# A Perceiver block with 6,272 keys: the second key half behind the second turns, value tiles elsewhere, moves in two parts, and the staging piece in front of the even context buffer

## The chip, the cores and the metric

The kernel runs on one core of one Trainium2 chip. The metric is the time of one execution in microseconds on the device; lower is better.

## The reference

A query of 64 rows of 512 numbers attends to 6,272 context rows of 512 (32 query heads of 128, 8 key and value heads). The result goes through a projection with bias, then through a block with weights kept as 4-bit codes with scales and low-rank parts (attention-like sum, gate and up, down), and a last layer with a Fourier transform of coefficients. The part that matters here, cut:

```python
q = (query @ Wq + bq).reshape(B, L, NKV, G, HDIM)
k_, v_ = jnp.split(kv @ Wkv + bkv, 2, axis=-1)
scores = jnp.einsum('blkgd,bmkd->bkglm', q, k) * scale
attn = jax.nn.softmax(scores, axis=-1)
o = jnp.einsum('bkglm,bmkd->blkgd', attn, v).reshape(B, L, NHEAD * HDIM)
return o @ Wo + bo
```

The 4-bit weights are expanded on the chip during the attention: codes become numbers (a maximum over straight lines), which are scaled and stored.

## The kernel before, in words

**Blocks and chunks.** The context is cut into NCH = 7 chunks of 896 keys (CT = 7 tiles of 128; two halves of 448). Each chunk passes 8 key heads; one chunk and one head make a block, i = 8 s + h, 56 in all (NB). A softmax that runs along with new maxima joins the chunks. Each float32 number is split in two parts (hi and lo), and each product is three matmuls (L86 to L90: hi by hi, hi by lo, lo by hi).

**The engines in a block.** Each engine has its own list, written out by hand, and runs it in order. PE (L944): the scores of the block in four pieces (two halves by two row tiles), the transposes ("turns") of the probabilities of the block before (turn_probs, four groups of up to two tiles), the keys of the next head in two halves (next_keys; the first into p_s, the second into p_kv), the product of values and probabilities (weigh_values, into p_o, in a part of tiles 0 to 3 and a part of 4 to 6), the value tiles of a pair of heads (value_tile, into the two banks of p_kv, 4 in even blocks and 3 in odd ones), and the turn of an output (turn_output). ACT (L1306) rounds what PE leaves in PSUM to the hi part, takes the exponentials (weigh), rounds pieces of the next chunk's context (round_ctx) and computes four of the eight lines of a weight tile. DVE (L1606) subtracts to get the lo parts (split_keys, split_values, split_probs), takes the score statistics, adds outputs, and merges lines (merge 0 to 5). GpSimd (POOL, L674) has the other lines, the lo part of context pieces (split_ctx), and joins and scales a weight tile (join). SP (L505) issues the loads.

**The moves.** The exponentials lie in probs. SP copies them by DMA to probs_r, one DMA for each of two row tiles, for the transposes to read (move_probs, L465). It first waits until all four turns of the block before have read probs_r (pt_psum, 4 i), and DVE may write probs again only when the copy has landed.

**The buffers.** The context of even chunks lies in ctx_even_hi and ctx_even_lo, that of odd chunks in ctx_odd_hi and ctx_odd_lo. While one chunk is worked on, the other buffer is filled in 16 pieces through one staging tile (ctx_st, 896 bytes in each partition), which lay between the two. ctx_piece (L71) says which piece goes at which of five places of a pair of blocks. The banks of p_kv are shared by keys, values and scores in turn. kv_number gives each use its number; PE waits on kv_split (DVE is through with that use), ACT and SP on kv_psum.

**The first blocks.** Blocks 0 to 2 also hold the rest of the query projection (query_product, query_turn on PE, query_out on ACT, finish_query on DVE) and the splitting of the key and value weights (round_wkv on ACT, split_wkv on DVE), with 1 MB loads of wq in the same queue.

## Time and profile before

| | us |
|---|---|
| median of 3 timed runs | 1011.46 |
| lowest and highest of them | 1010.75, 1011.51 |
| the profiled execution | 1011.92 |
| its span, first to last instruction | 1010.1 |
| PE busy in the span | 995.1 |
| DVE, ACT, POOL busy | 745.5, 586.5, 443.5 |

The profile is one execution. Each engine's busy time is the time in which it had an instruction under way. Matmuls overlap each other by their modelled ends, so that a busy PE can still stand for a short time: the distance from one start to the next tells more.

### The profile page before, as it was taken

What the parts mean: (1) busy time and instruction counts of PE and PEld (TensorE: products, weight loads), DVE (VectorE), ACT (ScalarE), POOL (GpSimd) and SP (SyncE); (2) the same over time, 40 slices, a digit from 0 to 9 for tenths busy, and PEclk for the clock granted to TensorE, in tenths of its full rate; (3) what the DMA queues carried; (4) which work ended last, traced back from release to release, by engine and by line L of the source; (5) the groups of instructions that cost most, each with busy time, mean ns of one, the idle gap of its engine ahead of it and who ended that gap; (6) DMA issues with size and microseconds to landing.
All of it is one profiled execution on the core that took longest, in us unless ns stands there. A gap on an engine that the chain in (4) does not pass through costs nothing.

```text
span 1010.1 us, 20355 instructions
## 1 busy us (share of the span) xinstructions
PE 995.1 (99%) x7083; PEld 921.6 (91%) x7083; DVE 745.5 (74%) x1680; ACT 586.5 (58%) x1254; POOL 443.5 (44%) x641
## 2 busy tenths in 40 slices
PE   8999999999999999999999999999999999999998
PEld 6779999999999999999999999999999999999744
DVE  5678878777777778777776778777777768676766
ACT  6466666666565656566565666656565655565431
POOL 2244553545534444345454444534444445333331
PEclk9999999999999999999999999999999999999999
DMA  9663333333324343243333334333333237464895
GB/s 324 226 223 130 124 129 132 109 134 108 124 94 134 119 135 135 96 134 108 131 106 116 114 132 137 116 119 108 130 107 134 97 124 249 158 223 153 235 351 166
DMA packets 90086, 149.59 MB, mean 148 GB/s; under 512 B 10529, under 2 KB 44977, under 8 KB 89985
## 3 DMA queue, kind: packets, MB, share of 16 engines
q1 hardware_dynamic: 88224, 146.42, 43.8%
q10 hardware_dynamic: 1424, 1.51, 0.4%
q8 instruction: 58, 0.95, 0.4%
q0 software_dynamic: 336, 0.35, 0.2%
q14 instruction: 44, 0.35, 0.1%
HBM read 82.97 MB, written 14.81 MB: 97 GB/s over the span
## 4 chain that ended last, share of the span: by engine, by line
PE 93%; DVE 3%; DMA 2%; issue 1%; SPq 0%; ACT 0%; DVEq 0%
PE p_kv L88 16%; PE p_kv L90 16%; PE p_kv L89 16%; PE p_s L88 7%; PE p_s L90 7%; PE p_s L89 6%; PE p_t L769 6%; PE p_o L88 5%; PE p_o L90 5%; PE p_o L89 5%; PE p_s L849 1%; PE p_ot L753 1%; DMA wkv_raw<-in_wkv 1%; PE p_o L783 1%; DMA probs_r<-probs 1%
## 5 line engine op out<-in xcount | busy, mean ns | idle before, releaser
L610 POOL TENSOR_SCALAR slots<-code 128x512 f32<-128x512 bf16 x232 | 148.7, 641 | 247.3 <-DVE slots L1466 162.4
L1210 ACT ACTIVATE pt_hi<-p_t 128x512 fp32r<-128x512 f32 x224 | 109.9, 542 | 113.6 <-PE p_t L769 107.9
L1466 DVE TENSOR_TENSOR slots<-slots 128x512 f32<-128x512 f32 x232 | 170.0, 733 | 1.6 <-POOL slots L610 1.5
L1239 ACT ACTIVATE slots<-code,drop_and_offsets 128x512 f32<-128x512 bf16 x232 | 158.6, 713 | 8.1 <-POOL code L606 4.1
L1198 ACT ACTIVATE v_hi<-p_kv 128x256 fp32r<-128x256 f32 x196 | 75.2, 384 | 139.6 <-PE p_kv L90 138.7
L630 POOL TENSOR_TENSOR slots<-slots 128x512 f32<-128x512 f32 x58 | 77.0, 1327 | 158.2 <-DVE slots L1466 158.2
L1430 DVE TENSOR_TENSOR pt_lo<-p_t,pt_hi 128x512 fp32r<-128x512 f32 x224 | 128.7, 614 | 5.9 <-ACT pt_hi L1210 4.9
L1415 DVE TENSOR_TENSOR v_lo<-p_kv,v_hi 128x256 fp32r<-128x256 f32 x196 | 83.1, 424 | 67.6 <-ACT v_hi L1198 64.8
L88 PE MATMUL p_kv<-wkv_hi,ctx_even_hi 128*128 128x256 f32 x448 | 129.1, 288 | 0.2 <-DVE v_lo L1415 0.2
L89 PE MATMUL p_kv<-wkv_lo,ctx_even_hi 128*128 128x256 f32 x448 | 126.0, 281 | 0.0
L90 PE MATMUL p_kv<-wkv_hi,ctx_even_lo 128*128 128x256 f32 x448 | 126.0, 281 | 0.0
L1280 ACT ACTIVATE probs<-probs,mins 128x896 f32<-128x896 f32 x112 | 115.5, 1038 | 0.0
L88 PE MATMUL p_o<-pt_hi,v_hi 128*128 128x256 f32 x392 | 111.2, 284 | 2.2 <-issue 2.2
L1417 DVE SCALAR_TENSOR_TENSOR k_lo<-p_kv,bk_sb,k_hi 128x448 fp32r<-128x448 f32 x56 | 38.3, 684 | 100.6 <-ACT k_hi L1198 100.6
L90 PE MATMUL p_o<-pt_hi,v_lo 128*128 128x256 f32 x392 | 111.1, 283 | 0.0
L89 PE MATMUL p_o<-pt_lo,v_hi 128*128 128x256 f32 x392 | 110.8, 283 | 0.0
L88 PE MATMUL p_kv<-wkv_hi,ctx_odd_hi 128*128 128x256 f32 x336 | 97.0, 289 | 0.0
L90 PE MATMUL p_kv<-wkv_hi,ctx_odd_lo 128*128 128x256 f32 x336 | 94.9, 283 | 0.0
L89 PE MATMUL p_kv<-wkv_lo,ctx_odd_hi 128*128 128x256 f32 x336 | 94.4, 281 | 0.0
L1198 ACT ACTIVATE k_hi<-p_kv,bk_sb 128x448 fp32r<-128x448 f32 x56 | 35.6, 635 | 91.4 <-PE p_kv L90 91.4
L88 PEld LDWEIGHTS p_kv<-wkv_hi,ctx_even_hi 128*128 128x128 f32 x448 | 84.5, 189 | 1.1 <-issue 1.1
L89 PEld LDWEIGHTS p_kv<-wkv_lo,ctx_even_hi 128*128 128x128 f32 x448 | 84.6, 189 | 0.0
(261 smaller groups left out, 2717.7 us busy)
## 6 DMA issues: line engine op xcount, KB each, us to landing
probs_r<-probs SPq DMA_DIRECT2D x110, 448.0 KB, 3.6
code<-in_codes SPq DMA_DIRECT2D x58, 256.0 KB, 3.8
scale<-in_scales SPq DMA_DIRECT2D x114, 128.0 KB, 3.1
expanded_weights<-slots SPq DMA_DIRECT2D x56, 256.0 KB, 2.1
ctx_st<-in_ctx_t SPq DMA_DIRECT2D x96, 112.0 KB, 3.0
ring_hi<-expanded_weights SPq DMA_DIRECT2D x22, 256.0 KB, 5.9
ring_lo<-expanded_weights SPq DMA_DIRECT2D x22, 256.0 KB, 6.0
wq_hi<-in_wq SPq DMA_DIRECT2D x4, 1024.0 KB, 7.2
```

The costliest lines, as they stand in the source:

```text
L88: nc.tensor.matmul(out, hi, rhi, start=start, stop=False)
L89: nc.tensor.matmul(out, hi, rlo, start=False, stop=False)
L90: return nc.tensor.matmul(out, lo, rhi, start=False, stop=stop)
L610: nc.gpsimd.tensor_scalar(slots[:, slot, :], code16[:], LINES[j][0], LINES[j][1], ALU.mult, ALU.add).then_inc(pool_lines, 1)
L630: nc.gpsimd.tensor_tensor(slots[:, 0, :], slots[:, 0, :], slots[:, 4, :], ALU.subtract).then_inc(joined, 1)
L1198: nc.scalar.activation(dst, src, ACT.Identity, bias=0.0 if bias is None else bias).then_inc(kv_rounded, 1)
L1210: nc.scalar.activation(pt_hi[:, at:at + n, :].rearrange("p t q -> p (t q)"), p_t[:, c % 2, 0:n * ROWS], ACT.Copy).then_inc(pt_rounded, 1)
L1239: nc.scalar.activation(slots[:, slot, :], code16[:], ACT.Identity, bias=offsets[:, k:k + 1], scale=LINES[j][0]).then_inc(act_lines, 1)
L1280: nc.scalar.activation(probs[:, r, :], probs[:, r, :], ACT.Exp, bias=mins[:, h, r, now:now + 1], scale=-1.0, accum_out=rowsum[:, h % 4, r: ...
L1415: nc.vector.tensor_tensor(dst, src, hi.bitcast(F32), ALU.subtract).then_inc(kv_split, 1)
L1430: nc.vector.tensor_tensor(pt_lo[:, at:at + n, :].rearrange("p t q -> p (t q)"), p_t[:, c % 2, 0:n * ROWS], pt_hi[:, at:at + n, :].rearrang ...
L1466: nc.vector.tensor_tensor(slots[:, slot, :], slots[:, slot, :], slots[:, other, :], ALU.max).then_inc(merged, 1)
```

## The change

1. **Staging tile.** ctx_st is allocated in front of ctx_even_hi and no longer behind ctx_even_lo. The even buffers move up by 896 bytes; the odd ones stay.
2. **Order.** On PE the second key half follows the second pair of turns directly. The three value tiles of odd blocks go ahead of these turns, the four of even blocks to the end of the block. ACT and DVE follow the same order. The scores' second half then waits for the last use of the banks (last_kv). turn_output(0) and add_output(0, 0) go from block 2 to block 3.
3. **Moves in two parts.** move_probs copies columns 0 to 511 (front, when the first two turns before have read them) and columns 512 to 895 (back, when all have), each with its own semaphore.
4. **Pieces and lines.** The context pieces go at other places of ACT's, POOL's and SP's lists, and in chunk 0 two pieces are moved ahead; POOL's first two lines are separated by a piece; PE waits for the new context in four steps.

The diff, cut to its core:

```diff
@@ ctx_piece
-        piece = (0, 1, PIECES, PIECES, 2)[place]
+        piece = (0, 1, PIECES, 2, 3)[place]
+    elif pair == 1 and place < 2:
+        piece = (4, PIECES)[place]
@@ kv_number
-                uses = keys[:1] + tiles[:SPLIT_TILE] + keys[1:] + tiles[SPLIT_TILE:]
+                uses = keys + tiles if i % 2 == 0 else keys[:1] + tiles + keys[1:]
...
+            last_kv[i] = len(kv_number) - 1
@@ v_bank
+            return (t + 1) % 2 if i % 2 == 0 else t % 2
@@ move_probs
                 if i > 0:
+                    sp.wait_ge(pt_psum, 4 * i - 2)
+                for r in range(RT):
+                    sp.wait_ge(exp_ready, 2 * i + 1 + r)
+                    sp.dma_start(probs_r[:, r, FRONT].bitcast(F32), probs[:, r, FRONT]).then_inc(front_moved, 16)
+                if i > 0:
                     sp.wait_ge(pt_psum, 4 * i)
                 for r in range(RT):
-                    sp.wait_ge(exp_ready, 2 * i + 1 + r)
-                    sp.dma_start(probs_r[:, r].bitcast(F32), probs[:, r]).then_inc(probs_moved, 16)
+                    sp.dma_start(probs_r[:, r, BACK].bitcast(F32), probs[:, r, BACK]).then_inc(back_moved, 16)
@@ SP, a pair of blocks
                     load(0)
                     move_probs(n)
+                    load(1)
                     codes_of(n + 2)
-                    load(1)
@@ POOL, a pair of blocks
                     last_lines(n)
-                    narrow(n + 1)
+                    if n == 0:
+                        narrow(1)
                     split(0)
+                    if n > 0:
+                        narrow(n + 1)
                     add_rowsum(n, 2 * pair)
                     split(1)
                     join(n)
+                    first_line(n + 1)
                     split(2)
-                    first_lines(n + 1)
+                    second_line(n + 1)
@@ PE scores
-                    pe.wait_ge(kv_split, (LAST_KV if i == NB - 1 and c == 1 else use) + 1)
+                    pe.wait_ge(kv_split, (last_kv[i - 1] if c == 1 else kv_number["k", i - 1, 0]) + 1)
@@ PE block_work
+                if i == 3:
+                    turn_output(0)
                 turn_probs(i - 1, 0)
                 turn_probs(i - 1, 1)
...
-                if h + 1 == NKV:
-                    pe.wait_ge(ctx_split, PIECES * (s + 1))
                 next_keys(i, h, half, 0)
                 weigh_values(i - 1, 0, SPLIT_TILE)
                 if i == 2:
                     query_product(7)
+                if i % 2 == 1:
+                    for t in value_tiles(i):
+                        value_tile(i, h, half, t)
                 turn_probs(i - 1, 2)
                 turn_probs(i - 1, 3)
                 if i > 2:
                     turn_output(i - 2)
-                for t in value_tiles(i)[:SPLIT_TILE]:
-                    value_tile(i, h, half, t)
                 next_keys(i, h, half, 1)
                 weigh_values(i - 1, SPLIT_TILE, CT)
-                if i == 2:
-                    turn_output(0)
+                if i % 2 == 0:
+                    for t in value_tiles(i):
+                        if i == 2 and t == 2:
+                            query_turn(7)
+                        value_tile(i, h, half, t)
@@ ACT block_work
                 round_probs(i - 1, 0)
                 round_probs(i - 1, 1)
+                if h % 2 == 1:
+                    round_ctx(s, h, half, 2)
+                elif h >= 2:
+                    round_ctx(s, h - 2, half, 4)
...
                 round_probs(i - 1, 2)
                 round_probs(i - 1, 3)
+                round_ctx(s, h, half, 0 if h % 2 == 0 else 3)
...
                 round_keys(i, h, 1)
                 if i == 1:
                     round_wkv(3)
+                    query_out(6)
                     lines(i + 1, 0, 2)
@@ DVE block_work, even blocks
+                    for t in value_tiles(i):
+                        split_values(i, t)
+                        if t < 3:
+                            merge(i, 3 + t)
+                        if t == 1 and i < NKV - 2:
+                            split_wkv(h + 2)
+                        if t == 2 and i == 2:
+                            finish_query(7)
```

In odd blocks DVE splits tiles 4 to 6 ahead of split_probs 2 and 3, with merges 2 to 4 between them; in chunk 0 split_wkv follows split_probs.

## Rows read from the trace of the kernel before

**Rows 1.** The page, busy time of each engine.

```profile
PE 995.1 (99%) x7083; PEld 921.6 (91%) x7083; DVE 745.5 (74%) x1680; ACT 586.5 (58%) x1254; POOL 443.5 (44%) x641
```

**Rows 2.** Waits of PE: releaser, us in total, times, longest us.

```profile
PE p_o L88 <- issue: 2.2, 2, 1.3
...
PE p_kv L88 <- DVE v_lo L1415: 0.2, 1, 0.2
```

**Rows 3.** Windows, one pair of steady blocks.

```profile
core 0: us, PE busy (x) PEld busy (x) DVE busy (x) ACT busy (x) POOL busy (x), PEclk, DMA share, GB/s
457.00:489.50 32.50, 32.50 (x233) 31.35 (x232) 24.35 (x56) 20.13 (x46) 15.74 (x24) 1.00 0.37 124
```

**Rows 4.** Windows of an even and an odd chunk, instructions that touch wkv_hi; columns without POOL.

```profile
294.50:424.50 130.00, 77.67 (x352) 57.26 (x352) 0.00 (x0) 0.00 (x0) 1.00 0.36 120
424.50:554.50 130.00, 77.79 (x352) 57.22 (x352) 0.00 (x0) 0.00 (x0) 1.00 0.36 120
```

**Rows 5.** Groups by form of the whole span, first key half.

```profile
L89 PE MATMUL p_s<-ctx_even_lo,wkv_hi 128*128 128x448 f32 x128 | 47.0, 367 | 0.0
...
L89 PE MATMUL p_s<-ctx_odd_lo,wkv_hi 128*128 128x448 f32 x96 | 34.9, 363 | 0.0
```

**Rows 6.** Timeline at the boundary of blocks 54 and 55.

```profile
932.82 0.38 ACT L1198 ACTIVATE v_hi<-p_kv 128x256 fp32r<-128x256 f32 x1 [1.03 <-PE p_kv L90]
...
934.04 0.36 PE L88 MATMUL p_s<-k_hi,q_hi 128*128 128x448 f32 x1
...
934.25 0.38 ACT L1198 ACTIVATE v_hi<-p_kv 128x256 fp32r<-128x256 f32 x1 [1.04 <-PE p_kv L90]
...
934.66 0.42 DVE L1415 TENSOR_TENSOR v_lo<-p_kv,v_hi 128x256 fp32r<-128x256 f32 x1 [1.00 <-ACT v_hi L1198]
...
935.14 0.19 PEld L88 LDWEIGHTS p_kv<-k_hi,q_hi 128*128 128x128 f32 x1
935.25 0.37 PE L88 MATMUL p_kv<-k_hi,q_hi 128*128 128x448 f32 x1
```

**Rows 7.** Timeline of DVE in block 2.

```profile
79.68 0.68 DVE L1466 TENSOR_TENSOR slots<-slots 128x512 f32<-128x512 f32 x1
80.28 1.22 DVE L1586 TENSOR_TENSOR wkv_lo<-wkv_raw,wkv_hi 128x1024 fp32r<-128x1024 f32 x1
81.42 0.48 DVE L1568 TENSOR_TENSOR q_f<-p_ot,bq_sb 128x128 f32<-128x128 f32 x2
...
83.58 0.41 DVE L1415 TENSOR_TENSOR v_lo<-p_kv,v_hi 128x256 fp32r<-128x256 f32 x1
```

**Rows 8.** Timeline of PE in blocks 1 and 2.

```profile
58.84 1.95 PE L783 MATMUL p_ot<-wq_hi,xt 128*64 128x256 f32 x16 [0.30 <-DMA wq_hi<-in_wq]
...
64.37 0.38 PE L793 MATMUL p_ot<-ident,q_part 128*128 128x128 f32 x2
65.44 0.88 PE L769 MATMUL p_t<-ident_r,probs_r 128*128 128x128 f32 x8 [0.69 <-DMA probs_r<-probs]
...
68.54 0.37 PE L90 MATMUL p_s<-ctx_even_hi,wkv_lo 128*128 128x448 f32 x1
70.17 0.36 PE L88 MATMUL p_o<-pt_hi,v_hi 128*128 128x256 f32 x1 [1.26 <-issue]
```

**Rows 9.** Timeline of the DMA issues of SP.

```profile
51.63 0.63 SPq L484 DMA_DIRECT2D wq_lo<-in_wq  x1
56.04 1.15 SPq L471 DMA_DIRECT2D probs_r<-probs  x2
...
58.60 1.35 SPq L434 DMA_DIRECT2D ctx_st<-in_ctx_t  x1
```

**Rows 10.** Timeline of ACT in block 2.

```profile
66.37 0.39 ACT L1228 ACTIVATE ctx_odd_hi<-ctx_st 128x224 fp32r<-128x224 f32 x1 [4.95 <-DMA ctx_st<-in_ctx_t]
...
68.16 1.07 ACT L1210 ACTIVATE pt_hi<-p_t 128x512 fp32r<-128x512 f32 x2
```

**Rows 11.** Landing times of the moves (tile probs_r) between 100 and 850 us.

```profile
DMA to landing us min/median/max: 2.8/3.6/5.0
```

More of the change, by code:

```diff
@@ L139, in perceiver_block @@
               w_base, b_base, enc, coefs, mask, fourier, ident_in, out, ident, acc, denom, mins, bk_sb, bv_sb, wkv_hi,
[L140 removed]
+              wkv_lo, q_hi, q_lo, ctx_st, even_hi, even_lo, where, sem, sb, psum)
         phase1.close()
@@ L617, in first_lines, with second_line @@
                 line(0, 0)
+            def second_line(n, first=False):
                 if not first:
@@ L1321, in block_work @@
+                if h % 2 == 1:
+                    if i > 1:
+                        lines(i + 1, 0, 2)
+                round_keys(i, h, 1)
                 if i == 1:
                     round_wkv(3)
-                if h % 2 == 1:
-                    round_ctx(s, h, half, 3)
-                for n, t in enumerate(value_tiles(i)[:SPLIT_TILE]):
-                    round_values(i, t)
-                    if n == 1 and i < NKV - 2:
-                        round_wkv(h + 2)
-                    elif n == 1:
-                        lines(i + 1, 0, 1)
-                    if n == 2:
-                        lines(i + 1, 0 if i < NKV - 2 else 1, 2)
-                    if h % 2 == 0 and n == 2:
-                        round_ctx(s, h, half, 1)
@@ L1335, in block_work @@
-                if i == 1:
-                    lines(i + 1, 0, 2)
-                round_keys(i, h, 1)
-                if i == 1:
-                    query_out(6)
-                for t in value_tiles(i)[SPLIT_TILE:]:
-                    round_values(i, t)
-                round_ctx(s, h, half, 2 if h % 2 == 0 else 4)
+                    query_out(6)
+                    lines(i + 1, 0, 2)
+                if h % 2 == 0:
+                    for t in value_tiles(i):
+                        round_values(i, t)
+                        if t == 0 and i < NKV - 2:
+                            round_wkv(h + 2)
+                        if t == 1:
+                            if i >= NKV - 2:
+                                lines(i + 1, 0, 1)
+                            round_ctx(s, h, half, 1)
+                        if t == 2:
+                            lines(i + 1, 0 if i < NKV - 2 else 1, 2)
@@ L1620, in block_work @@
                 split_keys(i, h, 0)
-                merge(i, 2)
-                split_probs(i - 1, 2)
-                split_probs(i - 1, 3)
-                if i == 1:
-                    split_wkv(3)
+                if h % 2 == 1:
+                    tiles = value_tiles(i)
+                    for n in range(CT - SPLIT_TILE):
+                        if tiles:
+                            split_values(i, tiles[n])
+                        if n == 0:
+                            merge(i, 2)
+                        elif n == 1:
+                            merge(i, 3)
+                            merge(i, 4)
+                    split_probs(i - 1, 2)
+                    split_probs(i - 1, 3)
+                    if 1 < i < NKV - 2:
+                        split_wkv(h + 2)
+                    else:
+                        merge(i, 5)
+                else:
+                    split_probs(i - 1, 2)
+                    split_probs(i - 1, 3)
                 if i == 6:
@@ L1631, in block_work @@
                     invert(h - 2)
-                tiles = value_tiles(i)[:SPLIT_TILE]
-                for n in range(3):
-                    if n < len(tiles):
-                        split_values(i, tiles[n])
-                    merge(i, 3 + n)
-                if 1 < i < NKV - 2:
-                    split_wkv(h + 2)
-                if i == 2:
-                    finish_query(7)
-                for t in tiles[3:]:
-                    split_values(i, t)
-                split_keys(i, h, 1)
-                if i == 2:
-                    add_output(0, 0)
-                for t in value_tiles(i)[SPLIT_TILE:]:
-                    split_values(i, t)
+                if h % 2 == 0:
+                    merge(i, 2)
+                split_keys(i, h, 1)
+                if i == 1:
+                    split_wkv(3)
+                if h % 2 == 1:
+                    if 1 < i < NKV - 2:
+                        merge(i, 5)
+                else:
+                    for t in value_tiles(i):
+                        split_values(i, t)
+                        if t < 3:
+                            merge(i, 3 + t)
+                        if t == 1 and i < NKV - 2:
+                            split_wkv(h + 2)
+                        if t == 2 and i == 2:
+                            finish_query(7)
             def last_block():
```

61 lines of the change are left out of this document (35 added, 26 removed).

## The prediction

> **What bounds the kernel now.** I read the page first: PE is busy 995.1 of 1010.1 us [rows 1]. No other engine is near its limit, so a change of order can gain only what PE loses. Then I asked what PE waits for: 2.2 us "issue" before p_o and 0.2 us for a v_lo [rows 2], and 0.7 us for the move of the probabilities [rows 8]. A matmul's modelled end hides a part of each wait, so for the rest I read starts. In the steady part PE is busy all of the time, 32.50 of 32.50 us for a pair of blocks at the upper clock level [rows 3]. So what can be won or lost lies (a) in the first blocks, where PE does stand, (b) in new waits that the order might bring 25 times over, (c) in how fast the matmuls follow each other.
>
> **The moved address (even buffer 896 B further on).** No instruction changes. Its only possible effect is on the pace. The chunk from 294.50 uses the even buffer, that from 424.50 the odd one, which keeps its address: for the matmuls that touch wkv_hi PE is busy 77.67 us in the one and 77.79 in the other [rows 4]. The buffers do differ, but by 0.12 us a chunk, with keys dearer in even (367 against 363 ns for the same form [rows 5]) and so something else dearer in odd. If even comes to behave as odd in all: 3.5 chunks by 0.12, +0.4 us. In the keys alone: 4 ns on 24 matmuls in each of 28 blocks, -2.7 us. I take 0, nearest to the whole-chunk rows.
>
> **The second key half behind the second turns.** 12 matmuls of 448 columns now follow transposes instead of value tiles (in odd blocks value tiles, transposes, keys). The first half already follows transposes, and its pace is what rows 5 show: 363 to 367 ns. One matmul behind the transposes is slow either way, the first value matmul before, the first key matmul now, so that price moves and does not go. The pace of 54 blocks by 12 such matmuls can change by the spread of 4 ns at most, 648 by 4 = 2.6 us up or down. I take -1.0: less than half of it, to the better side, since 363 is had behind transposes in the odd chunks.
>
> **Value tiles elsewhere: the new wait in steady blocks.** In even blocks the four tiles come last, and the next block's second-half scores write the banks that the last tiles used, so PE waits until DVE has read them (last_kv). The trace has this very pattern once, at the last block: first score matmul at 934.04, ACT rounds the tile at 934.25, DVE splits it at 934.66 for 0.42, to 935.08; the weight load comes at 935.14 and its matmul at 935.25 [rows 6], six steps of 0.20 behind 934.04. The load goes 0.1 us later than it could and nothing is lost. Elsewhere DVE and ACT must be free at that moment. Tiles come 1.43 us apart (932.82 to 934.25 in rows 6); DVE has a split and a merge for each, 0.42 + 0.68 = 1.10 us, and ACT a rounding of 0.38 and one line (0.7 us; two in chunk 0). Cost 0; from the other side 0.1 us for an exposed weight load, 25 times, +2.5 us.
>
> **Where it does cost: block 3.** In block 2 DVE also has split_wkv(4), 1.22 us, now behind tile 1, and finish_query(7), from 81.42 to 83.58, between tiles 2 and 3; it splits tile 3 only at 83.58 [rows 7]. Before, 12 key matmuls (2.4 us), 9 of p_o (1.1) and 6 of the scores (1.2) stood between tile 3 and the first need of its bank; now the last 1.2 alone. From the end of tile 0 (T): DVE splits and merges to T+1.6, splits tile 1 at T+2.0, merges and does split_wkv to T+4.2, tile 2 and its merge to T+5.1, finish_query to T+6.6 (1.5 us where POOL leaves it alone) or 7.3, tile 3 to T+7.0 or 7.7. PE would be at the second half at T + 3 x 1.43 + 1.2 = T+5.5. Block 3 stands 1.5 to 2.2 us; I take 1.7. Block 4 has a split_wkv but no finish_query: +0.1.
>
> **Moves in two parts, and the piece ahead of them.** PE loses in block 2: query_turn's transposes at 64.37, those of the probabilities at 65.44, where 0.1 to 0.2 is due: 0.9 us. And 68.54 to 70.17 where 0.20 is due: 1.4 us [rows 8]. The move was issued at 56.04, behind the last MB of wq (51.63), the context piece at 58.60 [rows 9]. ACT stood 4.95 us for this piece, until 66.37, and turned to the probabilities at 68.16 [rows 10]: the second stall is ACT's. After, load(3) takes that piece ahead of the moves, near 52.3, and the front part goes when exp is done, near 54.5. But the queue serves in order: wq_hi was there for PE at 58.84 [rows 8]; at 0.35 MB a us (3 us a MB, an estimate from the page's highest slices) the next MB is there at 61.8, the piece at 62.0, the front part at 63.5, the back part at 64.8. ACT now stands for the piece in front of the second keys, whose matmuls are over at 58.5: k_hi starts at 62.3, k_lo ends at 63.6, and PE, which wants it at 63.1, stands 0.5 us. On DVE split_wkv(3) ends at 65.1 and the score statistics start there, not at the 65.4 of before; ACT is through with the probabilities 1 us earlier, and the p_o of 70.17 starts at about 69.1. Gain 1.1 us; 2.3 if both stalls went, 0 if they only change places.
>
> **The steady moves.** The back part of an odd block waits for turns that now come behind three value tiles: 2.4 (scores) + 0.6 (turns) + 2.4 (keys) + 1.4 (p_o) + 4.3 (tiles) + 0.6 = 11.7 us into the block, issued by 12.9. A whole move lands in 2.8 to 5.0 us, median 3.6 [rows 11]: at 16.5, at worst 17.9. DVE writes the second half of probs 1.9 us into the next block, at 15.5 + 1.9 = 17.4, and its split of the probabilities has 0.7 us to spare before PE wants it. Codes, piece, tile_out and scales behind it in SP's queue shift by 4 us, with over 3 us of room in each. Cost 0; the other side, 0.3 us in each of 25 odd blocks, 7.5 us, holds only if the landings of now were all at the slow end. The Trainium skill, "DMA: Bandwidth & Descriptors", "Anatomy of one DMA", gives each DMA a fixed part of about 2 us, which speaks against two parts; no row here shows it alone. By it, were the two parts paid one behind the other, the landing would be 18.5 and each odd block would wait 0.4 us.
>
> **Smaller ones.** In block 7 the last context piece of chunk 0 is split at about 5.0 us, where PE asks for it: +0.2. The v_lo wait of block 50 [rows 2] is a backlog of DVE; tiles 3.5 us later are past it: -0.3. In the last pair join(54) and the ring loads behind it are 3 us later, their slots read over 10 us later: 0.
>
> **Sum.** -1.1 (block 2) + 1.7 (block 3) + 0.1 + 0.2 - 0.3 - 1.0 (pace) = -0.4. The profiled execution took 1011.92 us (span 1010.1), 0.46 over the timed median of 1011.46. So 1011.5 there, 1011.06 as a median: 1011.0. A measurement of this kernel can tell about 0.2%, 2 us, from no change.
>
> **Rivals.** *Faster, by pace*: the keys alone take the better pace, by the address (-2.7) and by the order (-2.6 in place of -1.0): at most -4.7, half as much is likelier, 1008.6. For it: the pace depends on something (rows 5). Against: whole chunks differ by 0.12 us (rows 4). By the Trainium skill, "SBUF — State Buffer", "Who interferes with whom", PE never waits on another engine's accesses; by that rule an address matters in nothing.
> *Slower, by the tail of the tiles*: if DVE or ACT come to the last tile later than in rows 6, the 0.1 us of room is gone and every further 0.1 us costs 2.5 us; 0.1 beyond it gives 1013.5, 0.15 gives 1015. For: the room is little. Against: 1.10 us of work in 1.43.
> *Slower, by the back part* landing late: 0.1 us in each odd block is 2.5 us, 1013.5 and more. It decides from a landing at 18.1 on.
> *No reach*: block 2's stalls come back in another place and block 3 stands 2.2: with a pace of 0, 0 + 2.2 + 0 = +2.2 on 1011.46 less 0.3, 1013.4.
>
> **Chances.** The forecast 0.32 and half of the last rival's 0.20 stay within 0.2%; the faster rival 0.34; the tail of the tiles 0.10, the back part 0.04, half of the last rival 0.10. So faster 0.34, same 0.42, slower 0.24. The range takes 1008.0, beyond the faster rival's likelier half, to 1014.5.
>
> **What the next profile would show.** Block 3 with a gap of 1.5 to 2.2 us ahead of its second-half scores, released by DVE's v_lo. In block 2 no DMA wait of p_t, and 1 us or less ahead of p_o. ACT idle for ctx_st once, 3 to 5 us, until about 62. Steady pairs at 32.4 to 32.6 us with PE busy throughout: one over 32.7 says that the tile tail or the back part waits. Key matmuls of the even chunks at 363 ns would speak for the address. I am wrong if pairs change by over 0.1 us, or if block 3 does not stand.

## The result, and the profile after

The kernel after takes 1016.57 us (median of 6 executions, 1015.16 to 1018.66); the kernel before takes 1011.49 beside it (6 executions, 1010.07 to 1012.81). The ratio is 1.0054, 95% interval 1.0042 to 1.0065: 5 us slower, where 1011.0 was forecast and 1014.5 was the upper end. The profiled execution, the longest of the six, took 1018.66 us with a span of 1016.9 (first to last instruction).

The profile page's engine row and PE's waits answer to [rows 1] and [rows 2]. PE is busy 2.8 us more than in the kernel before, and a single wait for v_lo takes 2.8 us.

```profile
PE 997.9 (98%) x7083; PEld 922.4 (91%) x7083; DVE 756.2 (74%) x1680; ACT 584.9 (58%) x1254; POOL 457.7 (45%) x641
```

```profile
PE p_kv L90 <- DVE v_lo L1445: 3.1, 2, 2.8
...
PE p_o L90 <- issue: 1.6, 2, 1.0
...
PE p_s L90 <- DVE probs L1484: 0.9, 1, 0.9
```

To place the loss I took, for each block, the time from its first matmul (`p_s<-k_hi,q_hi` in the timeline of PE) to that of the next block. The table has these lengths in us for the kernel before, the kernel after, and four kernels of the experiments below. Each column is one profiled execution. In the columns spread and last_mended the clock fell early in block 0, which took 1.6 us more for it.

```
block        before   after  join_late  spread  all_mended_no_shift  last_mended
0             29.16   29.14      29.14   30.72                29.15        30.72
1 and 2       36.19   36.39      37.05   38.56                34.16        34.66
3             15.60   20.28      16.62   15.71                15.72        15.76
4             17.02   16.92      16.92   17.37                17.44        17.03
5             15.52   16.12      16.10   15.52                15.52        15.59
7             15.48   15.90      15.90   15.91                15.78        15.51
8 to 49      682.84  683.88     683.89  683.86               682.73       682.97
50            17.42   17.02      17.02   17.02                16.97        16.97
```

From before to after the two profiled spans differ by 6.8 us, more than the medians (5.1): block 3 has 4.7 of it, blocks 8 to 49 together 1.0, block 5 0.6, block 7 0.4, the start and blocks 1 and 2 0.4; block 50 gives 0.4 back.

Block 3 in the timeline of PE. The last matmul of the first score half starts at 85.21 and the first of the second half at 88.36, where 0.20 is due. What is over the due distance from one start to the next is called a stand here: this one has 2.95 us, and DVE's v_lo ends it. Behind it the matmuls follow at 0.37 us instead of 0.20.

```profile
85.21 0.36 PE L92 MATMUL p_s<-k_hi,q_lo 128*128 128x448 f32 x1
88.36 0.74 PE L90 MATMUL p_kv<-k_hi,q_hi 128*128 128x448 f32 x1 [2.79 <-DVE v_lo L1445]
88.90 0.57 PE L91 MATMUL p_kv<-k_lo,q_hi 128*128 128x448 f32 x1
89.27 0.57 PE L92 MATMUL p_kv<-k_hi,q_lo 128*128 128x448 f32 x1
```

The windows of the same stretch say why: the granted clock is 0.51 from 88.30 to 91.00, which is the lower level (1.2 GHz), behind the stand. Of the block's 4.68 us more, 2.95 are the stand. The other 1.73 are nearly all the low clock: in whole_moves, an experiment below, the same stand came without the fall, and the block took 1.47 us less (18.81). The first of these rows is a steady pair, to set beside [rows 3]; the columns are those named there.

```profile
463.50:496.10 32.60, 32.60 (x233) 31.32 (x232) 24.89 (x56) 20.04 (x45) 16.77 (x24) 1.00 0.37 124
84.20:104.50 20.30, 17.51 (x114) 16.40 (x113) 16.90 (x36) 11.66 (x25) 8.29 (x11) 0.92 0.26 82
85.00:88.30 3.30, 0.57 (x3) 0.19 (x1) 3.23 (x6) 1.16 (x2) 2.93 (x3) 1.00 0.00 0
88.30:91.00 2.70, 2.64 (x8) 2.27 (x9) 1.72 (x7) 0.00 (x0) 0.20 (x1) 0.51 0.56 190
```

What DVE did before that v_lo, to set beside [rows 7]: the steps come in the forecast order, but the seventh query's finish (q_f, q_hi, q_lo) takes from 84.72 to 87.89, 3.2 us.

```profile
82.65 1.22 DVE L1616 TENSOR_TENSOR wkv_lo<-wkv_raw,wkv_hi 128x1024 fp32r<-128x1024 f32 x1
83.79 0.42 DVE L1445 TENSOR_TENSOR v_lo<-p_kv,v_hi 128x256 fp32r<-128x256 f32 x1
84.12 0.68 DVE L1496 TENSOR_TENSOR slots<-slots 128x512 f32<-128x512 f32 x1
84.72 0.48 DVE L1598 TENSOR_TENSOR q_f<-p_ot,bq_sb 128x128 f32<-128x128 f32 x2
85.23 1.17 DVE L1604 CAST q_hi<-q_f 128x256 fp32r<-128x256 f32 x1
86.43 1.54 DVE L1606 TENSOR_TENSOR q_lo<-q_f,q_hi 128x256 fp32r<-128x256 f32 x1
87.89 0.41 DVE L1445 TENSOR_TENSOR v_lo<-p_kv,v_hi 128x256 fp32r<-128x256 f32 x1
```

The merge at 84.12 is what POOL's join had waited for. The two steps of the join lie on q_hi and q_lo:

```profile
84.98 1.27 POOL L639 TENSOR_TENSOR slots<-slots 128x512 f32<-128x512 f32 x1 [6.66 <-DVE slots L1496]
86.43 1.26 POOL L648 TENSOR_TENSOR slots<-slots,scale 128x512 f32<-128x512 f32 x1 [0.18 <-POOL slots L639]
```

In blocks 1 and 2, ACT stands for ctx_st once, as forecast, and PE takes the probabilities without a wait for their move; but a `split_wkv` on DVE takes 2.30 us beside POOL's join, and the score statistics behind it come late. POOL's steps are at 64.24 and 65.72, the second with 2.04 us instead of 1.26. These rows answer to [rows 8] and [rows 10].

```profile
62.42 0.39 ACT L1246 ACTIVATE ctx_odd_hi<-ctx_st 128x224 fp32r<-128x224 f32 x1 [5.54 <-DMA ctx_st<-in_ctx_t]
```

```profile
64.32 2.30 DVE L1616 TENSOR_TENSOR wkv_lo<-wkv_raw,wkv_hi 128x1024 fp32r<-128x1024 f32 x1 [0.27 <-ACT wkv_hi L1290]
```

```profile
64.11 0.47 PE L90 MATMUL p_kv<-k_hi,q_hi 128*128 128x448 f32 x1 [0.35 <-DVE k_lo L1447]
67.31 0.44 PE L90 MATMUL p_s<-ctx_even_hi,wkv_hi 128*128 128x448 f32 x1 [0.88 <-DVE probs L1484]
```

### The profile page after: what moved, and what is told of

It reads as the page before. It is cut to its first block, busy times and chain, and to the rows that moved or that the text cites. A ratio compares the mean times of both kernels' runs of the same rounds, so it can differ in the third digit from the quotient of the medians.

```text
span 1016.9 us, 20498 instructions
## 1 busy us (share of the span) xinstructions
PE 997.9 (98%) x7083; PEld 922.4 (91%) x7083; DVE 756.2 (74%) x1680; ACT 584.9 (58%) x1254; POOL 457.7 (45%) x641
## 4 chain that ended last, share of the span: by engine, by line
PE 92%; DVE 3%; DMA 2%; issue 1%; ACT 1%; SPq 1%; POOL 0%; DVEq 0%; POOLq 0%; ACTq 0%
PE p_kv L90 16%; PE p_kv L92 16%; PE p_kv L91 15%; PE p_s L90 7%; PE p_s L91 6%; PE p_s L92 6%; PE p_t L785 6%; PE p_o L90 5%; PE p_o L92 5%; PE p_o L91 4%; PE p_s L865 1%; PE p_ot L769 1%; DMA wkv_raw<-in_wkv 1%; DMA ctx_st<-in_ctx_t 1%; PE p_o L799 1%
## 5 line engine op out<-in xcount | busy, mean ns | idle before, releaser
L617 POOL TENSOR_SCALAR slots<-code 128x512 f32<-128x512 bf16 x232 | 154.5, 666 | 137.5 <-DVE slots L1496 78.1
L1496 DVE TENSOR_TENSOR slots<-slots 128x512 f32<-128x512 f32 x232 | 173.0, 746 | 22.5 <-POOL slots L617 22.5
L1257 ACT ACTIVATE slots<-code,drop_and_offsets 128x512 f32<-128x512 bf16 x232 | 162.3, 718 | 21.7 <-POOL slots L639 18.3
L90 PE MATMUL p_kv<-wkv_hi,ctx_even_hi 128*128 128x256 f32 x448 | 126.8, 283 | 0.0
L90 PE MATMUL p_kv<-wkv_hi,ctx_odd_hi 128*128 128x256 f32 x336 | 94.8, 282 | 0.0
L1500 DVE SCALAR_TENSOR_TENSOR slots<-slots 128x512 f32<-128x512 f32 x116 | 84.8, 731 | 0.0
L92 PEld LDWEIGHTS p_kv<-wkv_hi,ctx_even_lo 128*128 128x128 f32 x448 | 84.0, 187 | 0.0
```

The costliest lines, as they stand in the source:

```text
L90: nc.tensor.matmul(out, hi, rhi, start=start, stop=False)
L92: return nc.tensor.matmul(out, lo, rhi, start=False, stop=stop)
L617: nc.gpsimd.tensor_scalar(slots[:, slot, :], code16[:], LINES[j][0], LINES[j][1], ALU.mult, ALU.add).then_inc(pool_lines, 1)
L1257: nc.scalar.activation(slots[:, slot, :], code16[:], ACT.Identity, bias=offsets[:, k:k + 1], scale=LINES[j][0]).then_inc(act_lines, 1)
L1496: nc.vector.tensor_tensor(slots[:, slot, :], slots[:, slot, :], slots[:, other, :], ALU.max).then_inc(merged, 1)
L1500: nc.vector.scalar_tensor_tensor(slots[:, slot, :], slots[:, slot, :], 0.0, slots[:, other, :], ALU.max, ALU.max).then_inc(merged, 1)
```

## The experiments

**How the times are to be read.** The executions of one kernel differ in their mean granted clock. Of the 23 of the kernel before that ran beside the first four experiments, 11 had 1.000 (median 1010.70) and 12 had 0.998 or 0.999 (1012.48). The traces show where the clock falls: in nine of the fourteen it is at its lower level for some 3.5 us between 18 and 24 us, and block 0 takes 30.6 to 31.3 us instead of 29.15. Elsewhere it falls only at a stand. The intervals below hold this scatter, so a difference under 1 us is read from the blocks of the traces, not from the medians. That also holds for the kernel after: 4 of its 6 executions had a clock of 1.000 (median 1016.28), so the low clock of block 3 is not in every one, and against the 1010.70 above the loss is 5.6 us without it.

**Theory and rivals.** Theory: DVE has a backlog at the end of block 2 (wkv split, query finish beside POOL's join), the stand of block 3 is that backlog and makes the clock fall; smaller waits of the same kind cost blocks 5 and 7; the rest is 1.0 us of pace, that is, of how fast the matmuls follow each other where nothing stands. Rivals: the moves in parts or the new order cost something everywhere; or the moved address does.

**query_last and join_late: the order on DVE, and POOL beside it.**

```diff
@@ query_last, DVE block_work
-                        if t == 2 and i == 2:
+                        if t == 3 and i == 2:
                             finish_query(7)
@@ join_late, DVE block_work
-                        if t < 3:
+                        if t < (2 if i == 2 else 3):
                             merge(i, 3 + t)
+                        if t == 3 and i == 2:
+                            merge(i, 5)
```

> The kernel after, with the seventh query's finish (turn with bias, rounding, low half, on DVE) moved in block 2 from behind the third value tile's split to behind the fourth's. Theory 1 (block 3's stand is the fourth tile's low half coming late behind that finish, and the low clock after it is the stand's result): the stand of 2.95 us shrinks to under 0.3 us, no stretch of block 3 has a granted clock near 0.5, block 3 goes from 20.3 us to 15.7 to 16.2, and the kernel to 1012.0 to 1012.8. Theory 2 (the time is lost all over, in the steady blocks' order and the moves in two parts; block 3 is one incident among others): the stand goes but blocks lose elsewhere, and the kernel stays at 1015 or more.

> The kernel after, with the last merge of block 2's lines (which releases POOL's join) moved behind the fourth tile's split; the seventh query's finish stays ahead of that split. It tells how much of the 3.2 us that the finish took is POOL working beside it. If POOL slows it: the finish takes 1.5 to 1.8 us, the stand in block 3 is 0.9 to 1.4 us instead of 2.95, and the kernel takes 1013.3 to 1014.8 (by whether the clock still falls behind a stand of 1 us). If the finish is as long alone: stand 2.5 us or more, 1016.0 to 1016.6.

Measured: query_last 1015.96 (ratio 1.0036, 1.0025 to 1.0048); join_late 1015.33 (1.0035, 1.0023 to 1.0048). By the ratios both give back nearly 2 us, by the medians 0.9 and 1.5, each less than forecast. Among executions with a clock of 1.000 the medians are 1015.43 and 1013.95 against 1016.28 of the kernel after. In join_late the finish takes 1.27 us instead of 3.2, with q_hi at 0.29 and q_lo at 0.43, and the stand is 0.37 us, less than I had expected:

```profile
84.51 0.48 DVE L1598 TENSOR_TENSOR q_f<-p_ot,bq_sb 128x128 f32<-128x128 f32 x2
85.02 0.29 DVE L1604 CAST q_hi<-q_f 128x256 fp32r<-128x256 f32 x1
85.35 0.43 DVE L1606 TENSOR_TENSOR q_lo<-q_f,q_hi 128x256 fp32r<-128x256 f32 x1
85.69 0.42 DVE L1445 TENSOR_TENSOR v_lo<-p_kv,v_hi 128x256 fp32r<-128x256 f32 x1
```

So POOL's join cost DVE 2.0 us there; the other 0.6 us that the stand lost is the merge itself, which the edit also takes from in front of the finish. The Trainium skill, "SBUF — State Buffer", "Who interferes with whom", says that a DVE instruction with two SBUF inputs, or a cast in a two-port mode, shares a port pair with GpSimd and blocks as a whole, while one with at most one SBUF input outside these modes does not; the trace agrees: q_f, with an input from PSUM, stays at 0.48 in both kernels.

In query_last block 3 still takes 16.80 us. The stand moved: PE comes to the output's matmuls before the probabilities are ready, since the score statistics start only behind the finish. It is 1.02 us from start to start where 0.20 is due.

```profile
92.06 0.36 PE L92 MATMUL p_s<-ctx_even_hi,wkv_lo 128*128 128x448 f32 x1
93.08 0.36 PE L90 MATMUL p_o<-pt_hi,v_hi 128*128 128x256 f32 x1 [0.66 <-issue]
```

**stage_alone and order_no_shift: the address by itself, in both orders.** The first is the kernel before with ctx_st allocated in front of ctx_even_hi; the second is the kernel after with ctx_st behind ctx_even_lo.

> The kernel before with one edit: the staging piece lies in front of the even context buffer, so all buffers behind it keep their order but the even pair starts one piece later. Theory A (the pair's address sets the pace): even chunks' and odd chunks' key projections get one spacing, and the time moves by up to 1 us. The prediction's sign: 1010.3 to 1010.8; the sign that the kernel after shows in blocks 8 to 49 (1.0 us longer): 1012.0 to 1012.8. Theory B (the order inside the blocks sets it, the address nothing): 1011.3 to 1011.7, and even and odd chunks still differ as before.

> The kernel after with the staging piece back behind the even buffer; new order and moves in two parts stay. Theory A (address sets the pace, and the shift cost the 1 us of blocks 8 to 49): 1015.3 to 1015.9, even and odd chunks differ again as in the kernel before. Theory B (the order cost it): 1016.4 to 1016.8, blocks 8 to 49 sum to 683.9 us as with the shift. The stand of block 3 is there in both.

Measured: stage_alone 1010.72 (0.9995, 0.9985 to 1.0004); order_no_shift 1015.55 (1.0038, 1.0025 to 1.0050). Neither interval can tell the address, so the pace is read from the traces.

order_no_shift shows something else as well. Its stand in block 3 is 1.86 us, not 2.95, with the same steps in the same order: q_hi is slow beside the join as before, but q_lo takes 0.42 us, and it is POOL's second step that is the longer one (1.57 instead of 1.26). The clock stays at 1.00 there, and the block takes 17.74 us, 2.15 more than before.

```profile
85.97 1.17 DVE L1604 CAST q_hi<-q_f 128x256 fp32r<-128x256 f32 x1
87.17 0.42 DVE L1606 TENSOR_TENSOR q_lo<-q_f,q_hi 128x256 fp32r<-128x256 f32 x1
```

```profile
87.16 1.57 POOL L648 TENSOR_TENSOR slots<-slots,scale 128x512 f32<-128x512 f32 x1 [0.18 <-POOL slots L639]
```

The first matmuls of blocks 8 and 50 give the pace of the 42 blocks between. The kernel before, then after, stage_alone and order_no_shift:

```profile
164.41 0.36 PE L88 MATMUL p_s<-k_hi,q_hi 128*128 128x448 f32 x1
...
847.25 0.36 PE L88 MATMUL p_s<-k_hi,q_hi 128*128 128x448 f32 x1
```

```profile
170.44 0.36 PE L90 MATMUL p_s<-k_hi,q_hi 128*128 128x448 f32 x1
...
854.32 0.36 PE L90 MATMUL p_s<-k_hi,q_hi 128*128 128x448 f32 x1
```

```profile
163.27 0.36 PE L88 MATMUL p_s<-k_hi,q_hi 128*128 128x448 f32 x1
...
845.63 0.36 PE L88 MATMUL p_s<-k_hi,q_hi 128*128 128x448 f32 x1
```

```profile
168.54 0.37 PE L90 MATMUL p_s<-k_hi,q_hi 128*128 128x448 f32 x1
...
851.43 0.36 PE L90 MATMUL p_s<-k_hi,q_hi 128*128 128x448 f32 x1
```

That is 682.84 and 683.88 us, 682.36 and 682.89. The shift takes 0.5 us off in the old order and adds 1.0 in the new one; the new order alone adds nothing (0.05). Other traces repeat the figures: with the new order and the shift five more have 683.79 to 683.90 (where the moves stay in two parts), with the new order and no shift two more have 682.73 and 682.97; for the shift in the old order there is one trace only. So theory A, that the address changes the pace, holds in each run, but not with one sign. With the shift all chunks are alike, a pair of blocks at 32.49 us in the old order and 32.57 in the new; without it their lengths differ from chunk to chunk (15.47 to 15.64 for an odd block of the kernel before). The odd chunks change too, though their own buffers stay where they are (from 130.04 to 129.97 us a chunk in the old order, from 130.16 to 130.26 in the new). Why the order decides what the shift gives, no run here tells.

**whole_moves and parts_alone: the moves in two parts.** whole_moves is the kernel after with each row tile moved by one transfer of 896 columns behind the fourth turn, with one semaphore for both halves of the statistics and for all turns; parts_alone is the kernel before with move_probs, DVE's wait and PE's wait as in the kernel after.

> The kernel after with each block's exponents moved in one part again, one transfer for each row tile; order and shift stay. Theory (the parts are hidden, as the prediction had it): within 0.5 us of the kernel after, 1016.1 to 1017.0. Rival (the parts cost DVE and SP time, or keep the even and the odd blocks' first transposes waiting): 1015.5 or less. Rival of the other sign (the new order needs the front part early, because the score statistics of the next block overwrite it): transposes or statistics wait by 0.2 us or more in each block, 1025 or more.

> The kernel before with the moves in two parts and nothing else. Theory (hidden, and its gain is the 0.7 us that the transposes of block 2 stood for the moved exponents): 1010.8 to 1011.8, and that stand is gone or under 0.2 us. Rival (four issues instead of two on SP delay the loads behind them): 1012.5 or more, with longer stands for query weights or context pieces in blocks 1 and 2.

Measured: whole_moves 1020.28 (1.0089, 1.0072 to 1.0106); parts_alone 1011.93 (1.0005, 0.9996 to 1.0014). The parts cost nothing alone, and in the new order they are needed: without them the median is 3.7 us higher. Part of that is clock, since none of the six executions of whole_moves had 1.000 and four of the kernel after did. The trace shows a mechanism in blocks 6 and 8, 1.5 us together, and nothing of it in the blocks behind; its execution was one of the shorter ones (1018.97), and where the rest goes in the longer ones stays open. The statistics, which overwrite the probabilities, wait 1.33 us for the whole move, and PE then stands before the output's matmuls, 0.64 us over its due distance in block 6, 0.70 in block 8.

```profile
138.69 0.62 DVE L1480 TENSOR_SCALAR_CACHE_REDUCE probs<-p_s 128x448 f32<-128x448 f32 x1 [1.33 <-DMA probs_r<-probs]
```

**pieces_back: the context pieces of the first two pairs.**

```diff
@@ ctx_piece
     elif pair == 0:
-        piece = (0, 1, PIECES, 2, 3)[place]
-    elif pair == 1 and place < 2:
-        piece = (4, PIECES)[place]
+        piece = (0, 1, PIECES, PIECES, 2)[place]
```

> The kernel after with the context pieces of the first two pairs in the places that they had before (the third piece is loaded in the last place of the first pair, the next two in the second pair's first). Theory (the earlier third piece keeps the one staging buffer, and ACT stands 5.5 us for it, which makes the low keys of block 1 late by 0.5 us and the scores' statistics by 1.0): blocks 1 and 2 together are 0.5 to 1.0 us shorter than the 36.4 of the kernel after, 1015.6 to 1016.1. Rival (it is the query weights' and probabilities' transfers that are late, whatever the pieces): 1016.4 to 1017.0.

Measured: 1016.03 (1.0047, 1.0031 to 1.0063), too wide an interval for 0.5 us. In the trace blocks 1 and 2 take 34.36 us instead of 36.39. That is more than forecast, and not all of it need be the pieces: the wait for the query weights at the end of block 1 differs between traces whose kernels do the same up to there (0.81 us over the due distance in the kernel after, 1.12 in join_late, 1.25 in query_last, 2.57 in spread, none in order_no_shift, where only an address is different), and in this trace there is none. Block 3 takes 20.68 us here: POOL's split of a context piece falls on the wkv split, which takes 1.70 us instead of 1.22, the stand grows to 3.42 us, and the clock falls with it.

**spread: the backlog taken apart.** In block 2 PE's query turn, ACT's wkv rounding and DVE's finish go ahead of the first tile, and the wkv split behind the first tile's split; in block 4 the two wkv steps do the same.

```diff
@@ DVE block_work, even blocks
+                    if i == 2:
+                        finish_query(7)
                     for t in value_tiles(i):
                         split_values(i, t)
+                        if t == 0 and i < NKV - 2:
+                            split_wkv(h + 2)
                         if t < 3:
                             merge(i, 3 + t)
-                        if t == 1 and i < NKV - 2:
-                            split_wkv(h + 2)
-                        if t == 2 and i == 2:
-                            finish_query(7)
```

> The kernel after with three of block 2's steps moved ahead of its value tiles (the wkv rounding on ACT and the seventh query's turn on PE ahead of the first tile, its finish on DVE ahead of the first tile's split, the wkv split behind that one; the wkv steps so in block 4 too). They fall into DVE's idle stretches of 1.6 us (78.7 to 80.3) and ACT's of 1.9 in the trace of the kernel after. Theory 1 (a backlog of DVE at the end of blocks 2 and 4 makes the stands of blocks 3 and 5, and moving one step of it behind the last tile only moved the stand to the output's matmuls): block 3 takes 15.6 to 15.9 us, block 5 15.5 to 15.7, and the kernel is 3.5 to 4.2 us shorter than the kernel after, 1012.3 to 1013.1. Theory 2 (the later score statistics and exponents of the new order would stand in the way in any case): block 3 stays at 16.6 or more and the kernel above 1014.

Measured: 1015.10 (1.0037, 1.0024 to 1.0050), above the 1012.3 to 1013.1 of theory 1; by the time alone it would speak for theory 2. The blocks do what theory 1 said, block 3 at 15.71 and block 5 at 15.52, while block 4 loses 0.45: its fourth tile now waits for DVE. The total does not follow in this execution (1017.67, the longest of five), because blocks 1 and 2 take 38.56. The wait for the query weights was 2.57 us over the due distance (2.42 in the row), and the clock fell behind it, in the windows 0.75 and then 0.65:

```profile
62.61 2.65 PE L799 MATMUL p_ot<-wq_hi,xt 128*64 128x256 f32 x16 [2.42 <-DMA wq_hi<-in_wq]
```

```profile
62.40:65.00 2.60, 2.39 (x16) 1.26 (x16) 0.00 (x0) 0.00 (x0) 0.00 (x0) 0.75 0.96 359
65.00:68.00 3.00, 3.00 (x15) 2.77 (x14) 1.36 (x2) 2.57 (x5) 1.72 (x4) 0.65 0.38 133
```

The run by itself therefore doesn't settle the sum; the next two do.

**all_mended and all_mended_no_shift: all causes taken away.** These are spread and pieces_back together, and this edit on POOL for block 7; the second has ctx_st behind the even buffer as well.

```diff
@@ POOL, a pair of blocks
                     join(n)
-                    first_line(n + 1)
-                    split(2)
+                    if s == 0 and pair == 3:
+                        split(2)
+                        first_line(n + 1)
+                    else:
+                        first_line(n + 1)
+                        split(2)
                     second_line(n + 1)
```

> The kernel after (shift kept) with three edits together: block 2's and 4's steps spread as in the run spread; the context pieces of the first two pairs placed as before, as in pieces_back; and in the first chunk's last pair POOL's third context split again ahead of the first line (it ended at 159.68 us and released block 7's keys 0.25 us late). Theory (the named incidents and 1.0 us of pace are all there is): blocks 3, 5 and 7 at 15.7, 15.5 and 15.5 us, blocks 1 and 2 together 34.4 to 36.2, the steady blocks 8 to 49 still at 683.7; 1011.0 to 1012.3. Rival (a general cost of the new order that no incident shows): 1013 or more.

> The same with the staging piece back behind the even buffer. Theory (in the new order the shift costs pace, in the old one it gives some): blocks 8 to 49 at 682.9 instead of 683.7, the rest as in all_mended; 0.8 to 1.0 us less, 1010.0 to 1011.4. Rival (the pace of the profile is hidden or made up elsewhere): the same time as all_mended.

Measured: all_mended 1012.31 (1.0006, 0.9997 to 1.0015), all_mended_no_shift 1011.30 (0.9992, 0.9983 to 1.0000), beside the same executions of the kernel before. So the named incidents and the shift are the loss: of 5 us, 4.3 to 4.8 go with the first kernel and 1.0 to 1.4 more with the second, whose blocks 8 to 49 take 682.73 us against 683.90 in the first. Only the POOL edit did nothing. Block 7 stays at 15.90: POOL's split waits for ACT's ctx_odd_hi, which ACT rounds in block 7 and rounded at the end of block 6 before.

**stands: what an idle time costs when it is made on purpose.**

```diff
@@ the kernel before
+AGAIN = {12: 3, 20: 4, 28: 6, 36: 8, 44: 10}
@@ DVE split_kv
                 dve.wait_ge(kv_rounded, use + 1)
+                for _ in range(again):
+                    nc.vector.tensor_reduce(scrap[:, len(used):len(used) + 1], src, AX_X, ALU.min)
+                    used.append(use)
@@ DVE split_keys
+                         AGAIN.get(i, 0) * c)
```

> The kernel before, with idle stands made on purpose in five steady even blocks: DVE reduces the key projection once more 3, 4, 6, 8 and 10 times ahead of the low keys of blocks 12, 20, 28, 36 and 44 (into columns that nobody reads), so that the next block's second half of scores stands for them, by an estimate of 0.5 us for each reduction less a cover of 0.9 us: 0.6, 1.1, 2.1, 3.1 and 4.1 us. It tells from which stand on the granted clock falls. Theory (the stand itself makes the clock fall, from about 2.5 us, as behind the 2.95 us of block 3): granted clock near 0.5 for some 3 us behind the two longest, 1.00 behind the three shorter; blocks 37 and 45 lose 1.4 to 1.8 us more than their stand; 1023 to 1027. Rival (the clock falls for what came before, the slow start of blocks 1 and 2, and a stand amid steady work costs its own length): 1.00 throughout, 1021 to 1023.

Measured: 1029.70 (1.0171, 1.0156 to 1.0186). The stands are 0.91, 1.44, 2.51, 3.57 and 4.63 us, 2 us more in all than estimated, and the kernel is above the 1027 of the theory. The blocks that hold them are longer than the odd blocks on either side (15.60 or 15.49) by 0.99, 1.62, 2.59, 6.05 and 6.62: the first three lose their stand and 0.1 to 0.2 us, the last two 2.5 and 2.0 us beyond it. The windows behind the third and the fourth stand show the clock at 1.00 in the one case and at 0.50, its lower level, in the other. There it had fallen before PE resumed at 648.11, and it was low until 653.5; behind the fifth stand PE resumed at 785.43 and the clock was low until 790.0. That is 5.4 and 4.6 us of work at half the clock, against 3.4 in block 3 of the kernel after, and the losses follow it.

```profile
514.80:518.00 3.20, 3.20 (x21) 2.95 (x21) 3.13 (x12) 1.56 (x4) 0.00 (x0) 1.00 0.01 2
644.30:648.00 3.70, 0.41 (x2) 0.02 (x1) 3.70 (x8) 0.56 (x2) 1.23 (x2) 0.82 0.55 174
648.00:651.50 3.50, 3.39 (x15) 3.03 (x15) 2.48 (x10) 0.28 (x1) 0.00 (x0) 0.50 0.00 0
651.50:655.00 3.50, 3.50 (x15) 3.16 (x14) 2.73 (x6) 2.96 (x7) 0.47 (x1) 0.72 0.00 0
```

So a stand amid steady work does bring the clock down, and the rival falls. The Trainium skill, "TensorE: Matmul & The Clock Gate", "HAM oscillation — how this bites in real kernels", says that waits of PE between stretches of matmuls throttle it and that each next stretch then starts at the lower clock; these rows agree. How long a stand has to be is not settled. The clock stayed up behind 2.51 us here, 1.86 in order_no_shift and 2.95 in whole_moves; it fell behind 2.57 in spread, 2.95 in the kernel after and 3.42 in pieces_back. So stands between 2.5 and 3 us did both.

**last_mended.** It takes up the two losses left in all_mended_no_shift: in block 4 the wkv split goes ahead of the first tile's split, and ACT rounds the last context piece of the first chunk at the end of block 6.

```diff
@@ DVE block_work, even blocks
                     if i == 2:
                         finish_query(7)
+                    elif i < NKV - 2:
+                        split_wkv(h + 2)
                     for t in value_tiles(i):
                         split_values(i, t)
-                        if t == 0 and i < NKV - 2:
+                        if t == 0 and i == 2:
                             split_wkv(h + 2)
@@ ACT block_work
                 if h % 2 == 1:
-                    round_ctx(s, h, half, 2)
+                    if i != 7:
+                        round_ctx(s, h, half, 2)
...
                     lines(i + 1, 3, 4)
+                    if i == 6:
+                        round_ctx(s, h, half, 2)
```

> The kernel of all_mended_no_shift with the two losses that its profile still shows taken up: in block 4 the wkv split goes ahead of the first value tile's split (there the fourth tile's matmuls stood 0.41 us for it; block 4 took 17.44 us), and ACT rounds the first chunk's last context piece at the end of block 6, as the kernel before does, instead of in block 7 (where POOL's split waited for ACT and PE's keys 0.25 us for POOL; that block took 15.78 us). Theory: block 4 at 17.0, block 7 at 15.5, in all 0.5 to 0.7 us less than all_mended_no_shift beside the same kernel before: a ratio of 0.9984 to 0.9990. Rival (the ACT step at the end of block 6 delays the score exponents of block 7 by as much): block 7 or 8 gains nothing, ratio 0.9990 to 0.9996.

Measured: 1009.43 us, 0.9980 of the kernel before beside it (1011.68), interval 0.9971 to 0.9989, a little better than forecast. This version beats both kernels, and at a clock of 1.000 as well (1009.42 against 1011.43). Blocks 4 and 7 are at 17.03 and 15.51, as forecast. Against the kernel before the gain lies in blocks 1 and 2 (34.66 us against 36.19) and block 50 (0.4); the steady blocks have none, and block 3 is 0.2 us longer. The windows of blocks 3, 4 and 7 show PE busy throughout at the upper clock:

```profile
83.70:99.50 15.80, 15.80 (x114) 15.07 (x113) 13.35 (x31) 11.30 (x24) 8.35 (x11) 1.00 0.35 114
99.50:116.50 17.00, 17.00 (x123) 16.28 (x123) 14.36 (x30) 10.30 (x23) 9.79 (x13) 1.00 0.37 126
149.00:164.50 15.50, 15.50 (x111) 14.83 (x110) 11.73 (x29) 9.90 (x22) 8.27 (x11) 1.00 0.37 117
```

## Why the prediction was wrong

**The term of block 3** is the step that failed, by size: 1.7 us was taken, 1.5 to 2.2 allowed, and block 3 grew by 4.7. The mechanism, its place and its releaser were right. Two things were missing. The finish was counted at 1.5 us, or 2.2 with POOL beside it, from [rows 7], where only q_lo was slow; where POOL's join would fall in the new order was not worked out. The merge that releases it comes just ahead of the finish, so the join fell on both steps that POOL can slow: 3.2 us, and 1.27 with the join elsewhere, as join_late shows. And the cost of a stand was taken as its length, when this one brought the lower clock, some 1.5 us more. Neither is in every trace of the same order: block 3 grew by 2.15 us in order_no_shift, where the join slowed one step only, inside the range that was allowed, and by 3.2 in whole_moves, where the clock stayed up. So the range held one of the outcomes that this order can have, and not the dearer ones.

**The term of blocks 1 and 2**, -1.1, came out at +0.2. The k_lo wait (0.5 forecast), ACT's long stand (until 62.42; 62.0 forecast) and the shorter stand before p_o were right. Two sizes were not. The wkv split was put at its length of 1.22 and took 2.30 beside POOL, which made the statistics start at 66.5 instead of the 65.1 named, and PE stand 0.88 us; and the query weights came 0.3 us later. pieces_back speaks for the moved context pieces as a part of it, without settling how much.

**The pace**, -1.0, came out at +1.0 over blocks 8 to 49, with the wrong sign. The order gave nothing, where I had -1.0, and the shift 1.0 more, where I had 0. The evidence that I used, 363 against 367 ns for one form [rows 5], was too small and too partial to give a sign. Nor does an address matter in nothing, as the prediction drew from a rule on engines waiting for each other's accesses; with the shift alone the pace changed in both orders. In the kernel after that form has 364 in even chunks and 365 in odd ones.

**Block 4's wkv split**, +0.1: the backlog shows in block 5, whose second score half waits 0.48 us for block 4's last tile; the split took 1.69 us, not 1.22, beside POOL's context split. Block 5 lost 0.6 and block 4 gained 0.1. **Block 7**, +0.2: +0.4, of which 0.25 stands at the place named. **Block 50**, -0.3: -0.4. **The tail of the tiles** and **the steady moves**, both 0: right; a steady pair takes 32.57 us with PE busy throughout, inside the 32.4 to 32.6 named. The 0.4 us for each odd block, worked out for two parts paid one behind the other, does not appear; the section of the Trainium skill from which the prediction took the fixed part ("DMA: Bandwidth & Descriptors", "Anatomy of one DMA") states it for transfers that GpSimd issues, and these are SP's. But parts_alone and whole_moves show that the two parts were not neutral in the new order: without them its median is 3.7 us higher.

So the sum of -0.4 was off by 3.0 us in block 3 (1.5 of it the clock, in some executions), 1.3 in blocks 1 and 2, 2.0 in pace and 0.5 in the backlog of block 4, 6.8 in all. The profiled execution is 7.2 above the sum's 1011.5, and the rest is 0.2 at the start and smaller blocks that nearly cancel. The median is only 5.5 above its 1011.06, as 4 of the 6 executions have no fall of the clock.

The rival "no reach" came nearest in kind, with stalls that come back elsewhere and 2.2 for block 3, and was too small for the same reason. "Slower, by the tail of the tiles" came nearest in time (up to 1015), but its mechanism did not occur. One working is off as well: half of the faster rival's -4.7 gives 1009.1, not 1008.6; that rival did not come.

## What to carry to other kernels

When a consumer is moved closer to its producer, list everything that the producing engine has queued ahead of that result, and also which other engine the last of these steps releases: its work may fall on the very instructions that are now urgent. Price a stand of the matmul engine of 2.5 us or more above its length (here 1.5 to 2.5 us above), since the clock may fall behind it. Where two engines slow each other, ask for both outcomes: the same order gave a stand of 1.86 us in one trace and 2.95 in another. Before a reordering is given up, see whether its losses are a few incidents in the first blocks: here they were but for 1 us of pace, and with these steps moved into idle time the new order won 0.2% over the old.

## What the runs showed of the hardware

- A DVE cast of 128x256 took 1.17 us instead of 0.29, and a subtraction with two SBUF inputs 1.54 instead of 0.43, beside POOL's 128x512 operations; q_f, with an input from PSUM, stayed at 0.48. In order_no_shift the subtraction kept its 0.42 and POOL's operation took 1.57 instead of 1.26.
- With stands of 0.91, 1.44 and 2.51 us the granted clock stayed at 1.00; with 3.57 and 4.63 us it was 0.50 for 5.4 and 4.6 us of the work behind and cost 2.5 and 2.0 us more than the stand. It fell with 2.57 (spread) and 3.42 us (pieces_back), and with 2.95 us in one trace of two.
- The staging tile in front of the even buffers, which lie 896 bytes further on for it, changed the time of 42 blocks by -0.5 us in one order and +1.0 us in the other, with no instruction changed.
